# Output products beside the masked maxima of a relational graph layer, spread column tiles, a last bias in TensorE's sums

## The chip, the cores and the metric

The kernel runs on one core of a Trainium2 chip. The metric is the device time of one execution in microseconds (us), as the median of several runs; less is better.

## The reference, cut to what matters

1250 nodes with 768 features and 40000 edges of three relations pass through one block. A layer norm feeds two branches: a graph attention of two layers (RGAT), and a linear attention with 12 heads. Their sum is added to x, and an int8 feed-forward with its own layer norm is added to that.

```python
xn = _layernorm(x)
# graph branch, layer by layer (4 heads of 192, then 1 head of 768)
xr = einsum('nd,rdf->rnf', x, W)          # 3 relations
alpha = leaky_relu((xr[etype, dst] @ q) + (xr[etype, src] @ k), 0.2)
m = segment_max(alpha, dst); e = exp(alpha - m[dst])
a = e / (segment_sum(e, dst)[dst] + 1e-16)
out = segment_sum(a * xr[etype, src], dst) + b      # elu between the layers
# linear attention: phi(q), phi(k), sums over nodes
y = (phi(q) @ (phi(k)^T v)) / (phi(q) @ sum phi(k)) ; mix = y @ W_out + b_out
x = x + gnn(xn) + mix
x_int8 = clip(round(_layernorm(x) / 0.02), -128, 127)
x = x + (x_int8 @ weight_t) * 0.0002 + bias
```

## The kernel before

Nodes lie in 10 blocks of 128 (NB), features in 6 blocks of 128 (K6), and columns of a product in halves of 384 (CW). A product of one block of nodes with one chunk of weights is 18 matmuls of 384 columns in fp16: for each of six k, high by high, high by low and low by high (line 1948 for x, lines 1743 to 1745 for the others). A chunk's high part is made on ScalarE (ACT, `w_hi_part`), its low part on VectorE (DVE, `w_lo_part`, line 1309). Products alternate between PSUM banks 6 and 7. Every engine's order is written out by hand, with semaphores between engines; all DMAs go through the SyncE queue (SP), in the order of its program.

The stages, in the order of the program, with the lines that the text names:

- **K, V**: products of the linear attention, with the edge counts built beside them. For each of 60 windows of 21 target nodes DVE makes one-hot tiles (lines 1283, 1284) and TensorE (PE) multiplies them, 14 matmuls a window here (line 1756, `count_window`). ACT evicts a window, and SP stores it to `ct_d`.
- **Q**: six blocks of q (line 1838, 72 matmuls of 320 columns), three windows each. After a block's products come three tiles of "weights times q, k" (`wq_tile`, line 1817): 12 small matmuls each, of 8 columns in fp32 (2 columns for layer 2), whose sums W q and W k stay in PSUM. 36 tiles in all: 21 by the end of this stage, 15 in the next.
- **Attention**: for each of 10 node blocks, PE transposes (1870), multiplies by phi(k)^T v (1859), counts a window (1756, for eight of the blocks) and takes one or two tiles (1817). DVE normalises (1400 to 1409) and makes `yt_lo` (1422) and one-hots.
- **Node columns**: xn times (W q, W k) gives every node's scores (1885 to 1887, `node_columns`), transposed to rows (1895). It waits for `wqk_lo` of DVE (1431, 1433).
- **Output products**: 20 products of the attention with W_out (chunks C_O, C_O + 1). DVE has added the summed bias to x in SBUF (1439, ten operations), and then adds each product to X (1448); SP stores X to `acc_d` (626) from where the last stage reloads it. After ten of them `node_values` (1908) spreads the scores of two heads.
- **Maxima**: 30 iterations w (NW). SP has loaded the counts CT from `ct_d` in five bulk loads (461). ACT turns two windows into a mask (991), PE transposes it (1934, `mask_rows`, ten transposes), ACT evicts it (1002), and DVE reduces scores plus mask for each of four heads (1461). Beside that PE makes the 60 products of x with the relations' weights: 36 matmuls first (S0), then 32 an iteration (SW), and 84 after the last. ACT evicts them (983, `xr_part`), SP stores them to `xr_d` (467), and also stores every mask (637) and loads the chunks (478, 1152 KB each).
- **Softmax tables** on DVE, stored and spread by a DMA (`tq_d`, 663, `load_table`), the first head's rows loaded (`load_head`, 485), `b1_bc` loaded (673) when all products are stored. Then four heads of exponentials, weights and aggregation (1054, 1059, 1548, 1552, 1985). DVE waits for `b1_in` before the first of them.
- **Layer 2** likewise (five groups of columns, 2042, 2043), its outputs added to `ac` from `acc_d` and stored to `y_d`.
- **Feed-forward**: SP loads eight of ten blocks of y in one DMA (767, 3024 KB) when the last store has landed; DVE takes their statistics (1248) and quantises (1658, 1660, 1662) within the last group. After the last group PE transposes (2086) and multiplies (2076, 12 matmuls a block, ten blocks of 126 rows); GpSimd (POOL) adds the bias to fx (868), DVE scales and adds (1698, `block_out`), SP stores.

The code on which the order around the change rests:

```python
S0 = 2 * PM; SW = 32; S1 = S0 + SW * NW          # PM = 18 matmuls of a product
def wq_load(t):                                  # three buffers wt
    if t >= 3:
        sp.wait_ge(wt_used, t - 2)
def product_steps(q0, q1):                       # PE, matmul q of the x products
    ...
    pe.wait_ge(g_free, 6 * NB + n + 1)           # the bank of two products ago
def xr_part(n):                                  # ACT evicts product n
    act.wait_ge(ev_out[n % 2], 16 * (n // 2) + 16)
    act.wait_ge(g_done, 6 * NB + n + 1)
def block_out(b):                                # DVE, last stage
    dve.wait_ge(fb_done, b + 1)                  # POOL's bias add
    dve.wait_ge(f_mm, b + 1)
```

Of the kernel before, what the change touches and what calls it, by code (L numbers as in the profile page):

```python
# [13 lines left out]
F32 = mybir.dt.float32  # L14
F16 = mybir.dt.float16
# [9 lines left out]
P = 128  # L25
# [43 lines left out]
PW = 25  # L69
PM = 3 * K6  # L70
S0 = 2 * PM
SW = 32
S1 = S0 + SW * NW
LO_AT = (0, 6, 12, 17, 23)
# [10 lines left out]
def build(nc, x, src, dst, et, W1, q1, k1, b1, W2, q2, k2, b2, Wqkv, bqkv, Wo, bo, wf, bf, W1t, W2t, out):  # L85
    ctx = ExitStack()
    with ctx:
# [45 lines left out]
        zrow = keep("zrow", [P, QH], F16, 2)  # L133
# [12 lines left out]
        QF = place("QF", [P, K6, NPAD], F32, 159984)  # L146
# [3 lines left out]
        yt_hi = place("yt_hi", [P, K6, NPAD], F16, 98304)  # L150
        yt_lo = place("yt_lo", [P, K6, NPAD], F16, 98304 + 15360)
# [12 lines left out]
        b2_bc0 = place("b2_bc0", [P, D], F32, 98304)  # L164
# [11 lines left out]
        CT = place("CT", [P, NWN, NB, R, WN], U16, 127008)  # L176
        assert 127008 + NWN * QN * 2 <= 202900
# [3 lines left out]
        kbc = place("kbc", [P, H, ND], F32, 91936)  # L181
        tt_junk = [place(f"tt_junk{j}", [P, ND], BF16, 112096 + 2528 * j) for j in range(H)]
# [54 lines left out]
        al2_2 = place("al2_2", [32, R, 1, WD], F32, 118400)  # L237
        mx_2 = place("mx_2", [32, 1, WD], F32, 118912)
        mx2_2 = place("mx2_2", [32, 1, WD], F32, 119104)
        tq2 = place("tq2", [32, 2, R, WD], F32, 119296)  # L240
        mk2 = [place(f"mk2_{j}", [P, 1], F32, 120320 + 32 * j) for j in range(2)]
# [3 lines left out]
        bf_bc = place("bf_bc", [P, D], F32, 9216)  # L245
# [23 lines left out]
        y_d = scratch("y_d", (ND, D), F32)  # L269

# [43 lines left out]
        acc_out = sem("acc_out")  # L314
# [33 lines left out]
        ct_in = [sem(f"ct_in{j}") for j in range(2)]  # L348
# [46 lines left out]
        fx_in = sem("fx_in")  # L395
# [5 lines left out]
        fb_done = sem("fb_done")  # L401
# [21 lines left out]

        def products_of(w):

            return range((S0 + SW * w) // PM, (S0 + SW * (w + 1)) // PM)

# [14 lines left out]

        def block_windows(i):

            return range(W_A + i, min(W_A + i + 1, NWN))

        def block_tiles(i):

            t = WT_TILES // 2 + 3
            return range(t + 2 * i, t + 2 * i + 2) if i < 5 else range(t + 5 + i, t + 6 + i)  # L450
# [81 lines left out]
        def _(sp):  # L532
# [49 lines left out]
            sp.dma_start(b2_bc0[:, :], b2.unsqueeze(0).to_broadcast([P, D])).then_inc(bias_in, 16)  # L582

# [1538 lines left out]
```

## Time and profile before

| | |
|---|---|
| median of 3 runs | 1767.53 us (1766.63 to 1769.37) |
| the profiled execution | 1774.47 us, its span 1772.5 us |
| PE busy | 1629.0 us (92% of the span) |
| DVE busy | 1321.3 us (75%) |
| ACT busy | 772.9 us (44%) |
| POOL busy | 156.7 us (9%) |
| DMA | 175.75 MB, 99 GB/s over the span |
| chain that ended last | PE 66%, DVE 15%, issue 10%, DMA 4%, ACT 2% |

The profiled execution is 1.97 us longer than its span, and 6.94 us longer than the median of the runs. A busy PE isn't PE at its peak: the clock that was granted (PEclk) stands beside it, and the ends of matmuls are modelled. The two lines of the page that give DVE and the clock in 40 slices of 44.3 us:

```profile
DVE  8699876757723999948899898972774377777786
PEclk9999998988898999979999999989999899999988
```

The maxima lie in slices 13 to 17, the heads of layer 1 in 18 to 27, the feed-forward in the last one.

### The profile page before, as it was taken

To read this page: it belongs to the slowest core of one execution; us is meant where nothing else is said; L and a number is where in the kernel's file an instruction comes from. 1 tells how busy PE (TensorE), PEld (TensorE's weight loads), DVE (VectorE), ACT (ScalarE), POOL (GpSimd) and SP (SyncE) were. 2 spreads that over 40 slices of the span, in tenths; PEclk is the share of its full clock that TensorE was granted. 3 is DMA by queue.
4 is the path that set the end of the run, shared out by engine and by line. 5 is a ranking of instruction groups with operands and counts; after the bars stand their busy time and mean duration, and the time that the engine had idled before them with its cause. 6 is when DMAs were issued, how large, how long until landed. Compare 5 with 4: busy or idle time off the path is not lost.

```text
span 1772.5 us, 34725 instructions
## 1 busy us (share of the span) xinstructions
PE 1629.0 (92%) x10527; PEld 1194.4 (67%) x10528; DVE 1321.3 (75%) x2631; ACT 772.9 (44%) x1021; POOL 156.7 (9%) x248
## 2 busy tenths in 40 slices
PE   4999999999898999959999999989899799999966
PEld 3566667778654666559999999976555455555534
DVE  8699876757723999948899898972774377777786
ACT  3331112322103665358888898862211233333342
POOL 2000000000000000000000000000000133333334
PEclk9999998988898999979999999989999899999988
DMA  5111132233353453451004132133664621101202
GB/s 195 31 60 57 60 94 81 76 103 104 102 230 131 143 167 118 138 167 59 29 29 124 53 109 75 36 98 94 187 192 139 225 88 53 36 17 53 105 22 87
DMA packets 122054, 175.75 MB, mean 99 GB/s; under 512 B 13090, under 2 KB 95678, under 8 KB 121458
## 3 DMA queue, kind: packets, MB, share of 16 engines
q1 hardware_dynamic: 121970, 174.68, 30.9%
q8 instruction: 46, 0.75, 0.2%
q14 instruction: 38, 0.31, 0.1%
HBM read 117.78 MB, written 56.87 MB: 99 GB/s over the span
## 4 chain that ended last, share of the span: by engine, by line
PE 66%; DVE 15%; issue 10%; DMA 4%; ACT 2%; DVEq 1%; POOL 1%; SPq 1%; ACTq 0%; POOLq 0%
PE ps L1985 21%; PE ps L2043 7%; PE ps L2042 7%; PE ps L1756 6%; PE ps L1743 5%; PE ps L1744 5%; PE ps L1745 5%; DVE tt_junk L1461 5%; PE ps L1838 3%; PE ps L1817 3%; DVE w_lo L1309 1%; DVE oh_q L1283 1%; PE ps L1799 1%; PE ps L1859 1%; DMA xr_d<-ev 1%
## 5 line engine op out<-in xcount | busy, mean ns | idle before, releaser
L1985 PE MATMUL ps<-xrh,pf 128*128 (+1 forms) x2400 | 400.0, 330 | 24.2 <-DVE pf L1552 24.2
L1985 PEld LDWEIGHTS ps<-xrh,pf 128*128 128x128 f32 x2400 | 393.6, 191 | 30.7 <-issue 28.4
L1743 PE MATMUL ps<-w_hi,xt_hi 128*128 128x384 f16 x600 | 198.7, 331 | 22.4 <-DVE ev L1599 14.0
L2042 PE MATMUL ps<-x,ph 128*128 (+1 forms) x600 | 196.6, 328 | 20.6 <-POOL pl L857 15.1
L1283 DVE TENSOR_SCALAR oh_q<-pat,codeT,neg_w 125x630 f16<-125x630 uint16 x420 | 185.9, 443 | 39.3 <-PE ps L1756 29.3
L1552 DVE SCALAR_TENSOR_TENSOR pf<-vb,CT 128x1260 f32<-128x1260 f32 x120 | 175.8, 1468 | 35.0 <-PE ps L1985 35.0
L1744 PE MATMUL ps<-w_lo,xt_hi 128*128 128x384 f16 x600 | 198.5, 331 | 0.0
L1745 PE MATMUL ps<-w_hi,xt_lo 128*128 128x384 f16 x600 | 198.2, 330 | 0.0
L2043 PE MATMUL ps<-x,ph 128*128 (+1 forms) x600 | 198.0, 330 | 0.0
L1548 DVE SCALAR_TENSOR_TENSOR vb<-vb,tb 128x1260 f32<-128x1260 f32 x120 | 173.1, 1466 | 29.4 <-DMA b_bc<-in_L_gnn_b 19.7
L1461 DVE CUSTOM_DVE_ANT_0 tt_junk<-kbc,mb 126x1260 bf16<-126x1260 f32 x120 | 168.3, 1465 | 20.6 <-issue 19.9
L1059 ACT ACTIVATE vb<-qbc,kcol 128x1260 f32<-128x1260 f32 x120 | 161.0, 1345 | 39.2 <-DVE pf L1552 37.8
L1054 ACT ACTIVATE tb<-qbc,kcol_leak 128x1260 f32<-128x1260 f32 x120 | 159.8, 1343 | 27.9 <-DVE vb L1548 20.6
L1756 PE MATMUL ps<-oh_q,oh_p 125*128 125x315 f16 x840 | 140.5, 321 | 8.8 <-DVE oh_p L1284 8.3
L1121 ACT ACTIVATE ph<-p 128x252 f16<-128x252 f32 x150 | 61.9, 413 | 161.3 <-PE ps L2043 156.0
L857 POOL TENSOR_TENSOR pl<-p,ph 128x252 f16<-128x252 f32 x150 | 110.8, 739 | 200.8 <-ACT ph L1121 189.5
L1948 PE MATMUL ps<-w_hi,xt_hi 128*128 128x384 f16 x360 | 118.6, 329 | 7.5 <-ACT ev L983 7.4
L1756 PEld LDWEIGHTS ps<-oh_q,oh_p 125*128 125x128 f16 x840 | 87.3, 106 | 52.2 <-DVE oh_p L1284 7.1
L1948 PE MATMUL ps<-w_hi,xt_lo 128*128 128x384 f16 x360 | 118.5, 329 | 0.0
L1948 PE MATMUL ps<-w_lo,xt_hi 128*128 128x384 f16 x360 | 118.5, 329 | 0.0
L1599 DVE TENSOR_TENSOR ev<-ps,ev 128x384 f16<-128x384 f32 x60 | 32.8, 556 | 97.5 <-ACT ev L1108 95.2
L1284 DVE TENSOR_SCALAR oh_p<-iota_l,sloT 125x128 f16<-125x128 f16 x420 | 105.4, 251 | 0.0
(226 smaller groups left out, 2436.8 us busy)
## 6 DMA issues: line engine op xcount, KB each, us to landing
qbc<-tq_d SPq DMA_DIRECT2D x12, 1260.0 KB, 6.4
xr_d<-ev SPq DMA_DIRECT2D x60, 192.0 KB, 2.0
xrh<-xr_d SPq DMA_DIRECT2D x4, 2880.0 KB, 14.8
x_d<-ev SPq DMA_DIRECT2D x60, 192.0 KB, 2.3
mb_d<-mb SPq DMA_DIRECT2D x30, 310.1 KB
mb<-mb_d SPq DMA_DIRECT2D x30, 310.1 KB
wst<-in_L_gnn_W SPq DMA_DIRECT2D x8, 1152.0 KB, 8.7
x<-x_d SPq DMA_DIRECT2D x2, 3840.0 KB, 19.0
```

The costliest lines, as they stand in the source:

```text
L1283: dve.tensor_scalar(oh_q[0:ET, u, :], pat[0:ET, :], codes[:, k:k + 1], neg_w[0:ET, ds(w, 1)], ALU.subtract, ALU.is_equal)
L1461: dve.tensor_tensor_reduce(out=tt_junk[k][0:WK, :], in0=kbc[0:WK, h, :], in1=mb[w % 2][0:WK, :], scale=1.0, scalar=2 * BIG, op0=ALU.subtra ...
L1548: dve.scalar_tensor_tensor(vb[j][:, :], vb[j][:, :], 2.0, tb[j][:, :], ALU.min, ALU.max).then_inc(v_step, 1)
L1552: dve.scalar_tensor_tensor(pf[j][:, 0:ND].rearrange("p (w d) -> p w d", d=WN), vb[j][:, :].rearrange("p (w d) -> p w d", d=WN), 2.0, CT[:, ...
L1743: pe.matmul(ps[:, bank, 0:CW], a_hi, hi[:, k, :], start=(k == 0), stop=False)
L1744: pe.matmul(ps[:, bank, 0:CW], a_hi, lo[:, k, :], start=False, stop=False)
L1745: last = pe.matmul(ps[:, bank, 0:CW], a_lo, hi[:, k, :], start=False, stop=(k == K6 - 1))
L1756: last = pe.matmul(ps[:, bank + q, 0:QH], oh_p[0:ET, u, :], oh_q[0:ET, u, q * QH:(q + 1) * QH], start=start, stop=False, skip_group_check= ...
L1948: mm = pe.matmul(ps[:, 6 + n % 2, 0:CW], a[:, k, i * P:(i + 1) * P], w[:, k, :], start=(q % PM == 0), stop=(q % PM == PM - 1))
L1985: mm = pe.matmul(out[b], pf[j][:, b * DB:b * DB + P], x, start=(first and b % 2 == 0), stop=False, skip_group_check=True)
L2042: pe.matmul(ps[:, bank, 0:CW], p, cols(off, off + CW), start=start, stop=False, skip_group_check=True)
L2043: mm = pe.matmul(ps[:, bank + 1, 0:CW + n1], p, cols(off + CW, off + D + n1), start=start, stop=False, skip_group_check=True)
```

## The change

Four things, with what goes with them.

1. **Tiles spread.** `wq_tile` now stands singly inside the steps k of a q block (`step_tile`), at most one a step: 3, 5, 5, 5, 4 and 4 tiles in the six blocks (Q_TILES), 26 in the stage, and one for each of the ten attention blocks.
2. **x stored in the attention.** The ten additions of the bias to X are made by DVE in the last three q blocks, and SP stores all of X to `acc_d` during the attention blocks. X need not stay in SBUF; yt, CT, kbc and others move.
3. **Output products streamed.** All 80 products are one sequence (NE): six stand first (PRE), among node columns, rows and `node_values`; then 36 matmuls an iteration instead of 32; 252 matmuls after the last iteration instead of 84. For the 20 output products a ring of four buffers `oa` takes the place of X: SP loads a piece of `acc_d` (`load_o`), DVE adds the product (`o_out`), SP stores it (`store_o`). 15 of the 20 `o_out` stand between the reductions of iterations 0 to 7. CT is loaded in pieces (two windows, six, six, and then two an iteration), the chunks in six pieces of 192 KB, two an iteration.
4. **Last stage.** The feed-forward bias is split in three bf16 terms and added by one matmul with six rows per half (constants 8 and 4992, times 0.0002 is 1); POOL's ten additions go. Transposes and products of blocks 0 and 1 stand inside the last relation of the last group, in banks 4 to 7. fx comes in two loads of four blocks, the first without a wait for the stores of the fourth group. DVE's wait for `b1_in` moves to where b1 is first used.

```diff
-S0 = 2 * PM
-SW = 32
+S0 = PRE * PM
+SW = 2 * PM
 S1 = S0 + SW * NW
-LO_AT = (0, 6, 12, 17, 23)
+LO_AT = (3, 8, 13, 18, 23, 28)
+CT_EARLY = 14
...
+        Q_TILES = (0, 3, 8, 13, 18, 22, 26)
...
+        def load_o(sp, n):
+
+            c, i = n // NB, n % NB
+            if n >= 4:
+                sp.wait_ge(oa_out[n % 4], 16 * (n // 4))
+            sp.dma_start(oa[n % 4][:, :], acc_d[i * P:(i + 1) * P, c * CW:(c + 1) * CW]).then_inc(oa_in[n % 4], 16)
+
+        def store_o(sp, n):
+
+            c, i = n // NB, n % NB
+            sp.wait_ge(g_free, 4 * NB + n + 3)
+            sp.dma_start(acc_d[i * P:(i + 1) * P, c * CW:(c + 1) * CW], oa[n % 4][:, :]).then_inc(oa_out[n % 4], 16)
...
             for i in range(NB):
+                sp.wait_ge(xb_done, i + 2)
+                sp.dma_start(acc_d[i * P:(i + 1) * P, :], X[:, i, :]).then_inc(xs_out, 16)
...
             def store_product(n):
 
-                sp.wait_ge(g_free, 6 * NB + n + 3)
-                store_xr(sp, n // NB, n % NB, n % 2)
+                if n < 2 * NB:
+                    store_o(sp, n)
+                    if 4 <= n + 2 < 2 * NB:
+                        load_o(sp, n + 2)
+                else:
+                    sp.wait_ge(g_free, 4 * NB + n + 3)
+                    store_xr(sp, n // NB - 2, n % NB, n % 2)
...
+            def o_out(n):
+
+                dve.wait_ge(oa_in[n % 4], 16 * (n // 4 + 1))
+                dve.wait_ge(g_done, 4 * NB + n + 1)
+                dve.tensor_tensor(oa[n % 4][:, :], ps[:, 6 + n % 2, 0:CW], oa[n % 4][:, :], ALU.add).then_inc(g_free, 1)
...
             for w in range(NW):
+                if PRE - 1 + 2 * w < 2 * NB:
+                    o_out(PRE - 1 + 2 * w)
                 dve.wait_ge(mb_done, w + 1)
                 for k, h in enumerate(range(H - 1, -1, -1)):
+                    if k == 2 and PRE + 2 * w < 2 * NB:
+                        o_out(PRE + 2 * w)
...
             def block_out(b):
-                dve.wait_ge(fb_done, b + 1)
                 dve.wait_ge(f_mm, b + 1)
...
                 for hf in range(2):
+                    pe.matmul(ps[0:DB, 4 + 2 * j + hf, 0:CW], bone[:, 0:DB], brow[:, hf * CW:(hf + 1) * CW], start=True, stop=False)
                     for k in range(K6):
```

How the instructions move. On PE in the first q block, the tiles of weights times q, k (`qkn,wt`) before stand together between the last products (`xt`,`w`) and a window (`oh_q,oh_p`):

```order
L1838 MATMUL ps<-xt_hi,w_hi_80 128x320 x4
L1838 MATMUL ps<-xt_lo,w_hi_80 128x320 x4
L1838 MATMUL ps<-xt_hi,w_lo_82 128x320 x4
L1817 MATMUL ps<-qkn,wt_105 128x2x4 x6
L1817 MATMUL ps<-qkn,wt_106 128x2x4 x6
L1817 MATMUL ps<-qkn,wt_107 128x2x4 x6
L1756 MATMUL ps<-oh_q,oh_p 128x315 x8
```

The same place now (the lines are those of the changed file):

```order
L1885 MATMUL ps<-qkn,wt_110 128x2x4 x6
L1911 MATMUL ps<-xt_hi,w_hi_84 128x320 x4
L1911 MATMUL ps<-xt_lo,w_hi_84 128x320 x4
L1911 MATMUL ps<-xt_hi,w_lo_86 128x320 x4
L1885 MATMUL ps<-qkn,wt_111 128x2x4 x6
L1911 MATMUL ps<-xt_hi,w_hi_84 128x320 x4
L1911 MATMUL ps<-xt_lo,w_hi_84 128x320 x4
L1911 MATMUL ps<-xt_hi,w_lo_86 128x320 x4
L1824 MATMUL ps<-oh_q,oh_p 128x315 x8
```

Between two tiles there are now 12 matmuls of 320 columns. On DVE after the attention, before:

```order
L1422 TENSOR_TENSOR yt_lo<-ps,yt_hi 128x3x128 x2
L1309 TENSOR_TENSOR w_lo_83<-wst_79,w_hi_81 128x2304
L1431 TENSOR_TENSOR wqk_lo<-ps,wqk_hi 128x144
L1433 TENSOR_TENSOR wqk_lo<-ps,wqk_hi 128x36
L1436 COPY kcol<-ps 128x240
L1439 TENSOR_TENSOR X<-X,bsum 128x768 x10
```

and now, up to the first reductions (`tt_junk`), with the four ring buffers oa_133 to oa_136:

```order
L1490 TENSOR_TENSOR yt_lo<-ps,yt_hi 128x3x128 x2
L1499 TENSOR_TENSOR wqk_lo<-ps,wqk_hi 128x144
L1501 TENSOR_TENSOR wqk_lo<-ps,wqk_hi 128x36
L1508 TENSOR_TENSOR oa_133<-ps,oa_133 128x384
L1512 COPY kcol<-ps 128x240
L1371 TENSOR_TENSOR w_lo_87<-wst_83,w_hi_85 128x2304
L1508 TENSOR_TENSOR oa_134<-ps,oa_134 128x384
...
L1529 ISA tt_junk_142,mkt<-kbc,mb_139 126x1260
L1529 ISA mkt 126x1
L1529 ISA tt_junk_143,mkt<-kbc,mb_139 126x1260
L1529 ISA mkt 126x1
L1508 TENSOR_TENSOR oa_135<-ps,oa_135 128x384
```

The second low part stands behind `wqk_lo`, the ten additions to X are gone from here, and the additions of products stand between reductions. On SP, where bulk loads of CT and of a chunk stood ahead of the first products' stores, before:

```order
L610 DMA kq_d<-kq 24x1280
L478 DMA wst_78<-in_L_gnn_W 128x6x384
L461 DMA CT<-ct_d 128x5040
L461 DMA CT<-ct_d 128x12600 x2
L478 DMA wst_79<-in_L_gnn_W 128x6x384
```

stands now, at the start of iteration 0 of the maxima:

```order
L669 DMA mb_d<-mb_139 126x1260
L516 DMA acc_d<-oa_134 128x384
L510 DMA oa_136<-acc_d 128x384
L503 DMA wst_82<-in_L_gnn_W 128x384
L516 DMA acc_d<-oa_135 128x384
L510 DMA oa_133<-acc_d 128x384
L516 DMA acc_d<-oa_136 128x384
L510 DMA oa_134<-acc_d 128x384
L481 DMA CT<-ct_d 128x1260
```

Stores, reloads, mask stores and pieces of CT take turns in one queue.

## Rows read from the trace of the kernel before

**Rows 1.** Windows view, core 0: stretch, its us, busy by engine, clock, DMA share, GB/s
```profile
260.87:396.28 135.41, 135.41 (x931) 101.65 (x929) 90.05 (x294) 37.75 (x68) 1.88 (x1) 0.87 0.31 98
396.28:440.60 44.32, 42.37 (x297) 38.25 (x298) 33.49 (x118) 8.75 (x16) 0.00 (x0) 0.83 0.33 95
464.50:482.30 17.80, 13.40 (x227) 9.79 (x226) 12.69 (x16) 2.01 (x6) 0.00 (x0) 0.66 0.25 75
543.00:568.13 25.13, 18.45 (x100) 10.09 (x97) 8.31 (x11) 10.91 (x12) 0.00 (x0) 0.87 0.50 163
568.13:744.73 176.60, 174.32 (x1240) 111.09 (x1240) 172.14 (x294) 101.21 (x115) 0.00 (x0) 0.99 0.42 133
744.73:774.54 29.81, 8.41 (x52) 5.03 (x53) 9.11 (x20) 9.21 (x10) 0.26 (x4) 0.69 0.85 245
1726.20:1765.30 39.10, 29.14 (x180) 22.71 (x180) 29.45 (x40) 11.07 (x14) 21.54 (x14) 0.83 0.26 88
```

**Rows 2.** Timeline of PE, two stretches: start, us, line, operation, count
```profile
292.34 4.76 PE L1817 MATMUL ps<-qkn,wt 128*128 128x8 f32 x36
296.96 3.85 PE L1756 MATMUL ps<-oh_q,oh_p 125*128 125x315 f16 x14
...
424.16 2.81 PE L1859 MATMUL ps<-kvd,QF 128*128 128x130 f32 x12
...
441.29 1.51 PE L1859 MATMUL ps<-kvd,QF 128*128 128x130 f32 x12
442.64 2.08 PE L1756 MATMUL ps<-oh_q,oh_p 125*128 125x315 f16 x14
...
444.58 1.48 PE L1817 MATMUL ps<-qkn,wt 128*128 128x2 f32 x12
```

**Rows 3.** Timeline of DVE around the end of the attention
```profile
443.37 1.02 DVE L1409 TENSOR_TENSOR yn<-ps,rdn 128x384 f32<-128x384 f32 x2
...
449.38 1.02 DVE L1409 TENSOR_TENSOR yn<-ps,rdn 128x384 f32<-128x384 f32 x2
...
461.83 2.55 DVE L1309 TENSOR_TENSOR w_lo<-wst,w_hi 128x2304 f16<-128x2304 f32 x1
```

**Rows 4.** Timeline of PE, the node columns' first matmul
```profile
468.16 0.20 PE L1885 MATMUL ps<-wqk_hi,xt_hi 128*128 128x24 f16 x1 [3.65 <-DVE wqk_lo L1433]
```

**Rows 5.** Timeline of DVE in the output products
```profile
489.27 0.56 DVE L1448 TENSOR_TENSOR X<-ps,X 128x384 f32 x1 [2.39 <-PE ps L1745]
```

**Rows 6.** Timeline of ACT at the start of the maxima
```profile
567.58 0.49 ACT L983 ACTIVATE ev<-ps 128x384 f32<-128x384 f32 x1 [9.08 <-DMA xr_d<-ev]
```

**Rows 7.** Timelines of POOL, ACT and DVE before the first head
```profile
753.34 0.16 POOL L834 MEMSET xrh<- 128x30 f32 x1 [294.17 <-PE ps L1948]
...
764.77 2.58 ACT L1054 ACTIVATE tb<-qbc,kcol_leak 128x1260 f32<-128x1260 f32 x2 [5.71 <-DMA qbc<-tq_d]
...
770.16 2.85 DVE L1548 SCALAR_TENSOR_TENSOR vb<-vb,tb 128x1260 f32<-128x1260 f32 x2 [19.72 <-DMA b_bc<-in_L_gnn_b]
```

**Rows 8.** Timeline of DVE in the last group
```profile
1683.03 1.02 DVE L1248 BATCH_NORM_STATS2 stat<-fx 126x6 f32<-126x384 f32 x2 [4.75 <-DMA fx<-y_d]
```

**Rows 9.** Timelines of DVE and PE in the last stage
```profile
1743.36 2.04 DVE L1662 TENSOR_SCALAR fn<-fn 126x768 f32<-126x768 f32 x1
...
1746.95 0.56 DVE L1660 TENSOR_SCALAR fn<-fn 126x768 f32<-126x768 f32 x1
...
1764.29 1.02 DVE L1698 SCALAR_TENSOR_TENSOR fx<-ps,fx 126x384 f32<-126x384 f32 x2 [0.93 <-PE ps L2076]
...
1757.83 2.12 PE L2076 MATMUL ps<-wf,fqt 128*126 128x384 f16 x12
```

**Rows 10.** DMA issues: count, KB each, median us from issue to landing
```profile
wst<-in_L_gnn_W SPq DMA_DIRECT2D x24, 192.0 KB, 2.5
...
acc_d<-X SPq DMA_DIRECT2D x20, 192.0 KB, 2.8
...
CT<-ct_d SPq DMA_DIRECT2D x1, 315.0 KB, 3.2
```

More of the change, by code:

```diff
@@ L313, in build @@
         xb_done = sem("xb_done")
-        acc_out = sem("acc_out")
+        xs_out = sem("xs_out")
+        oa_in = [sem(f"oa_in{j}") for j in range(4)]
+        oa_out = [sem(f"oa_out{j}") for j in range(4)]
         qkn_in = sem("qkn_in")
@@ L347, in build @@
         ct_out = [sem(f"ct_out{j}") for j in range(2)]
-        ct_in = [sem(f"ct_in{j}") for j in range(2)]
+        ct_in = [sem(f"ct_in{j}") for j in range(4)]
         mt_done = sem("mt_done")
@@ L394, in build @@
         wf_done = sem("wf_done")
-        fx_in = sem("fx_in")
+        fx_in = [sem(f"fx_in{q}") for q in range(2)]
+        bf_step = sem("bf_step")
+        bf_st = sem("bf_st")
+        br_in = sem("br_in")
         f_step = sem("f_step")
@@ L1020, in _ @@
                     xr_part(n)
-            for n in range(S1 // PM, 2 * R * NB):
+            for n in range(S1 // PM, NE):
                 xr_part(n)
@@ L1394, in _ @@
                     count_part(W_Q + 3 * (3 * c + fb) + 3)
+                    if c == 1:
+                        for u in range(3):
+                            dve.tensor_tensor(sub(X, 3 * fb + u), sub(X, 3 * fb + u), bsum[:, :], ALU.add).then_inc(xb_done, 1)
+            dve.tensor_tensor(X[:, NB - 1, :], X[:, NB - 1, :], bsum[:, :], ALU.add).then_inc(xb_done, 1)
             def normalised(i):
@@ L1514, in head_scaled @@
                     dve.wait_ge(h_st, 32 * h)
+                elif blocks[0] == BLOCKS[0]:
+                    dve.wait_ge(b1_in, 16)
                 for b in blocks:
@@ L2044, in unit_products2, with ffn_product, ffn_transposes @@
                 mm.then_inc(mm_done, 1)
+            def ffn_product(b):
+                j = b % 2
+                pe.wait_ge(f_cp, b + 1)
+                if b >= 2:
+                    pe.wait_ge(f_out, 2 * (b - 1))
+                for hf in range(2):
+                    pe.matmul(ps[0:DB, 4 + 2 * j + hf, 0:CW], bone[:, 0:DB], brow[:, hf * CW:(hf + 1) * CW], start=True, stop=False)
+                    for k in range(K6):
+                        mm = pe.matmul(ps[0:DB, 4 + 2 * j + hf, 0:CW], fqt[j][:, k, 0:DB], wf16[:, k, hf * CW:(hf + 1) * CW],
+                                       start=False, stop=(k == K6 - 1))
+                mm.then_inc(f_mm, 1)
+            def ffn_transposes(b, bank):
+                pe.wait_ge(fq_done, b + 1)
+                for k in range(K6):
+                    last = pe.transpose(ps16[:, bank, k * DB:(k + 1) * DB], fq[b][0:DB, k * P:(k + 1) * P], ident16[0:DB, 0:DB])
+                last.then_inc(f_tr, 1)
             for g in range(NG):
```

354 lines of the change are left out of this document (184 added, 170 removed).

## The prediction

> **What bounds the kernel now.** I first read the page's chain that ended last: PE has 66% of it, DVE 15%, issue 10%. PE is busy 92% of the span, so time can go in two ways only: PE's idle time, or stretches in which PE is busy at less than full clock. The windows view shows where each lies [rows 1]: the columns to read are the length, PE's busy time, DVE's and the clock. The Q stage has no idle PE but a clock of 0.87; attention blocks 0 to 4 have both faults; the next four stretches lack 4.4, 6.7, 2.3 and 21.4 us of PE (length less busy); the last stage lacks 10.0. Then the timelines name what ended each wait [rows 2 to 9]. The heads of layer 1 and layer 2's groups are hardly edited, and are taken over unchanged.
>
> **Term A, Q stage.** The tiles of weights times q, k come in bursts of three, 36 small matmuls in 4.76 us, and the window behind such a burst takes 3.85 us where the same 14 matmuls take 2.08 later [rows 2]: half speed (1.2 of 2.4 GHz). The granted clock falls in or behind the burst. Seven bursts cost about 7 x 1.65 = 11.5 us that way (1.77 here, a little less in the others) (the clock of 0.87 would by itself allow 135.4 x 0.13 = 17.6, but the tiles' own time hardly depends on it). Single tiles between 12 matmuls each should not lower it; I take that from blocks 7 to 9 of the attention, where one tile of 1.48 us stands beside a window of 2.08 and 12 products in 1.51 (2.81 in the blocks with two tiles) [rows 2]. Against it stand five more tiles here, 5 x 1.35 = 6.7 us (a third of 4.0 to 4.8), and 1 us where DVE's ten additions to X, now under the last q blocks, hold up a one-hot: -11.5 + 6.7 + 1, **-4** (bounds +6, no clock gained and all added, and -8).
>
> **Term B, attention.** Blocks 0 to 4 with two tiles take 44.3 us [rows 1]: 4 to start and 5 of about 8. With one tile PE needs some 5.3 us a block at full clock, and DVE, which normalises and makes one-hots, 6.01 (449.38 less 443.37, from one block's `yn` to the next, in which DVE had no pause) [rows 3]. DVE becomes the limit: 4 + 5 x 6.0 = 34, **-10.3**; two later blocks that ran at 5.3 have a tile's worth more to share the clock with, +1. SP stores X here (3.8 MB at 95 GB/s already moving): nobody waits for these stores before the first reload. Net **-9.3** (bounds 0 and -12).
>
> **Term C, node columns to first head.** What goes, by stretch of rows 1:
> - 464.5 to 482.3: PE waits 3.65 us for `wqk_lo` [rows 4], because a `w_lo` of 2.55 stands ahead of it on DVE [rows 3]. It now stands behind. 4.4 less 0.8 for a wait of its length: -3.6.
> - 543 to 568: ACT waits 9.08 us for the store of `ev` [rows 6], which stands on SP behind two bulk CT loads and a whole chunk. These become pieces: -6.7, and 1 more for the clock of 0.87.
> - 568 to 744.7: its 2.3 us of idle.
> - 744.7 to 774.5: after the last product (the POOL memset at 753.34 marks it) ACT waits for `qbc` until 764.77, and DVE for `b_bc` until 770.16 [rows 7], the end of a queue that is 0.85 busy. Tables, head load and the new place of the `b1_in` wait now lie under 252 matmuls, 41 us at 0.163, instead of 84, 13.7. Left are an eviction of 0.5, four exponentials of 1.3 (half of 2.58), `vb` 1.43 (half of 2.85) and `pf` about as long, together about 8.8: -12.6.
>
> That is -26.2. The additions that leave the output stage free nothing on PE: there a product takes 2.95 us (2.39 waiting, 0.56 adding) [rows 5], which is 18 matmuls of 0.163, PE's own pace. All 80 products remain, and move only.
>
> What it adds: an iteration of maxima is 6.09 us now (176.6/29), 5.4 for 33 matmuls and 0.65 for ten transposes. With 36 matmuls PE needs 6.5. DVE spent 172.14 us in 29 iterations, with five `w_lo` of 2.55: (172.14 - 12.75)/29 = 5.5 for four reductions; two additions of 0.56 make it 6.6, with semaphores 6.8. So iterations 0 to 7 go at DVE's pace, 0.3 x 7.5 = 2.3 us more; the `w_lo` of iteration 3, 2.55 us, finds PE only one bank ahead, and I take 1.2 of it. Later iterations are PE's, 6.5 against 5.8 with a slack that takes each `w_lo` in. SP has also to wait for `tq` tables with stores queued behind it: products 71 to 79 stand there, and I take 2 us (nothing to 6). Net **-21** (bounds -12 and -26.2).
>
> **Term D, fx in two loads.** DVE's 4.75 us before the first statistics [rows 8] were one load of 3024 KB that waited for the last store of the fourth group. The first half now waits for older stores: **-4** (0 to -4.75).
>
> **Term E, last stage.** `fn` takes 2.04 us beside POOL's additions and 0.56 without [rows 9]; the 21.54 us of POOL [rows 1] go. A block is 12 matmuls of 384 columns in 2.12 us; two bias matmuls more, 14 x 0.163 + 0.33 for transposes = 2.6 a block. Two of ten blocks stand ahead, inside the last group, where PE waits for POOL's `pl` in any case. From the last group's end (about 1728, two us into the stretch) that is 8 x 2.6 = 21, plus about 2.5 of eviction: the last `block_out` ends near 1751.6 rather than at 1765.3 [rows 9]: **-13.5** (bounds -8, if DVE's work on quantising, 29.45 us in the stretch, takes PE's place as the limit, and -16).
>
> **Sum.** -4 - 9.3 - 21 - 4 - 13.5 = -51.8, say -51.5. Against the profiled execution of 1774.5 us this is 1723; the median of the runs lies 6.94 below that execution, so the forecast is **1716**. A measurement of this kernel tells about 0.2% (3.5 us) from no change.
>
> **A rule weighed.** The tables show 192 KB pieces landing 2.5 us after issue and ring stores of 2.8 [rows 10]. The Trainium skill, "DMA: Bandwidth & Descriptors", section on measured rates and its two cost components, says to batch transfers to at least 1 MiB, and that a transfer costs about 2.0 us fixed; that speaks against this change, which cuts 1152 KB chunks into six and adds a ring of 384-column pieces. By that figure a piece of 192 KB is estimated at 2.45 us, with which the trace agrees (2.5); six in turn would be 14.7 where one whole would be 4.7. What the rule would make of the time is the third rival below, in rows of this case.
>
> **Rivals.**
> 1. *The clock does not come back.* A tile itself, not the row of three, may be what lowers it, and there are five more in the Q stage. For it: the stretch 464.5 to 482.3 ran at 0.66 with no tile at all. Against it: the blocks with one tile [rows 2]. A and B shrink from -13.3 to -2: 1727 us. Chance 0.12.
> 2. *The ring is late.* In iterations 0 to 7 an iteration moves 2 x 192 KB in, 2 x 192 out, CT 315, the mask 310 out and chunk pieces, 230 on the mean: 1.6 MB in 6.5 us, 250 GB/s, where 133 are moved now and 245 at a DMA share of 0.85 [rows 1]. A buffer comes round in four products, 12.9 us, for store and reload; if in a full queue each of them takes as long as the longest wait now, 9.1 us [rows 6], a round is 5.3 longer, and four rounds (16 products) +21: 1737. Against it: 2.8 + 2.8 us unloaded [rows 10]. Chance 0.15.
> 3. *Slower: transfers in turn.* If each one waits for the one ahead, an iteration of the first eight is 2 x 2.8 + 2 x 2.8 for the ring, 3.2 for CT, 3.2 for the mask and 1.2 x 2.5 for pieces = 20 us rather than 6.5; 13.5 x 7.5 = +101, which gives 1817. The change turns from gain to loss where an iteration passes 6.5 + 51.5/7.5 = 13.4 us. For it: ring, CT and mask share SP's one queue. Against it: in 568 to 744.7 us two stores, a mask store and pieces would sum to over 8 us an iteration by the same count, and the pace is 6.09. Chance 0.03. (The rule of the Trainium skill, "DMA: Bandwidth & Descriptors", on small transfers points this way; no row here shows a queue in which they take full turns.)
> 4. *It does nothing of weight*, the gains at the node columns and the last stage being taken up by the next wait in both places, 1755 to 1775: 0.04.
>
> **The numbers.** The forecast as worked out has 0.66. Its bounds: A and B each 4 to 9 off, C 9, E 5.5, which do not fall together; the square sum is about 14. The range of **1702 to 1737** takes in rivals 1 and 2 and leaves out 3 and 4 and the ends of the forecast's own spread. Faster by over 0.2%: 0.66 + 0.12 + 0.15 and a quarter of rival 4, **0.94**; the same **0.02**, from rival 4; slower, rival 3 and the rest of rival 4, **0.04**.
>
> **What would show it.** Right: granted clock near 1.00 in Q and attention; attention blocks about 6.0 us apart; no wait of 3.65 us ahead of the node columns; iterations of maxima 6.5 to 6.8 us, and no addition waiting for a DMA; PE's gap between last product and first head about 9 us; no wait at the first fx statistics; `fn` near 0.56 throughout and a last stage of about 26 us rather than 39. Wrong: a clock under 0.95 in Q (A, B); DVE waiting for `oa` loads, or PE for banks with DVE idle (C); PE waiting for DVE's quantised blocks at the end (E).

## The result, and the profile after

The changed kernel takes 1757.15 us, the median of 18 runs (1752.94 to 1770.71), where the kernel before takes 1770.37 (18 runs, 1766.51 to 1775.91). The ratio is 0.9934, with a 95% interval of 0.9917 to 0.9951: faster, by 0.7%, about 12 us (the two medians are 13.2 apart), rather than the 51.5 us that were forecast. The forecast of 1716 was wrong, and so was its range, which ended at 1737. The profiled execution has a span of 1758.5 us, 14.0 less than before.

The windows view of the changed kernel, cut at the same places of the program as [rows 1] (columns as there): the Q stage, the attention up to the node columns' place, the products and maxima up to the first head, layer 1's end to layer 2's first group, the groups, and the last stage.

```profile
260.90:414.59 153.69, 135.13 (x992) 100.92 (x991) 96.75 (x303) 37.08 (x68) 2.76 (x6) 0.94 0.33 100
414.60:473.00 58.40, 52.71 (x422) 46.23 (x420) 55.20 (x184) 15.11 (x29) 2.20 (x9) 0.97 0.47 141
473.00:768.16 295.16, 274.86 (x1960) 170.73 (x1959) 206.63 (x351) 128.92 (x143) 0.26 (x4) 0.96 0.58 176
1170.30:1402.30 232.00, 202.14 (x1334) 123.08 (x1334) 117.99 (x246) 60.60 (x103) 2.08 (x11) 0.93 0.51 154
1402.30:1716.70 314.40, 303.56 (x1823) 178.29 (x1824) 241.41 (x524) 121.18 (x306) 116.18 (x164) 0.98 0.20 66
1716.70:1758.50 41.80, 30.80 (x179) 19.79 (x177) 22.40 (x49) 10.71 (x13) 1.48 (x4) 0.90 0.27 92
```

The same stretches of the kernel before:

```profile
260.80:396.14 135.34, 135.34 (x933) 101.55 (x931) 90.12 (x294) 37.75 (x68) 1.88 (x1) 0.87 0.31 98
396.14:464.50 68.36, 64.96 (x482) 58.66 (x480) 54.46 (x182) 15.21 (x29) 2.20 (x9) 0.87 0.31 92
464.50:774.50 310.00, 274.50 (x1959) 170.86 (x1958) 215.74 (x360) 126.36 (x142) 0.26 (x4) 0.93 0.48 158
1177.20:1405.90 228.70, 200.57 (x1334) 122.66 (x1334) 117.42 (x245) 60.47 (x102) 1.42 (x10) 0.94 0.53 156
1405.90:1721.60 315.70, 300.61 (x1797) 176.33 (x1797) 241.28 (x523) 119.36 (x304) 116.46 (x165) 0.98 0.19 67
1721.60:1772.50 50.90, 29.96 (x185) 23.02 (x183) 33.82 (x51) 12.68 (x16) 21.54 (x14) 0.81 0.23 76
```

Set beside the terms of the prediction, these lengths give:

| stretch | forecast | change of its length |
|---|---|---|
| A, Q stage | -4 | **+18.4** |
| B, attention | -9.3 | -10.0 |
| C, node columns to first head | -21 | -14.8 |
| heads (402.7 to 402.1) and the way to layer 2's groups | 0 | +2.7 |
| D, groups of layer 2 | -4 | -1.3 |
| E, last stage | -13.5 | -9.1 |
| sum | -51.8 | -14.1 |

Nearly the whole shortfall of 38 us lies in A (22), C (6) and D with E (7). The first row is the one to read twice: PE is busy for as long as before (135.13 and 135.34 us), at a higher clock (0.94 for 0.87), which has paid for the five tiles more; but 18.6 us of idle time have come into a stage that had none. The waits view of PE names them, for the changed kernel in the Q stage (in the kernel before it is empty there):

```profile
PE ps L1824 <- DVE oh_p L1346: 12.3, 12, 5.6
PE ps L1911 <- DVE q_t L1451: 5.4, 5, 1.1
```

The timeline of PE shows where one block of q hands over to the next, and the end of the last block:

```profile
277.17 0.43 PE L1911 MATMUL ps<-xt_hi,w_hi 128*128 128x320 f16 x2
278.69 0.77 PE L1911 MATMUL ps<-xt_hi,w_hi 128*128 128x320 f16 x2 [1.09 <-DVE q_t L1451]
...
284.27 0.72 PE L1824 MATMUL ps<-oh_q,oh_p 125*128 125x315 f16 x4 [0.24 <-DVE oh_p L1346]
285.82 0.99 PE L1824 MATMUL ps<-oh_q,oh_p 125*128 125x315 f16 x6 [0.83 <-DVE oh_p L1346]
...
312.86 1.23 PE L1911 MATMUL ps<-xt_hi,w_hi 128*128 128x320 f16 x4
...
317.40 0.70 PE L1911 MATMUL ps<-xt_hi,w_hi 128*128 128x320 f16 x4
...
410.47 2.26 PE L1824 MATMUL ps<-oh_q,oh_p 125*128 125x315 f16 x8 [5.64 <-DVE oh_p L1346]
```

and the timeline of DVE at such a place what it does meanwhile:

```profile
377.92 1.01 DVE L1451 TENSOR_SCALAR q_t<-ps,bq_col 128x320 f32<-128x320 f32 x2 [3.02 <-PE ps L1911]
379.62 0.49 DVE L1456 SCALAR_TENSOR_TENSOR QF<-q_t,q_m 128x320 f32 x1 [0.69 <-ACT q_m L996]
...
383.44 0.49 DVE L1456 SCALAR_TENSOR_TENSOR QF<-q_t,q_m 128x320 f32 x1 [0.37 <-ACT q_m L996]
384.49 0.45 DVE L1345 TENSOR_SCALAR oh_q<-pat,codeT,neg_w 125x630 f16<-125x630 uint16 x1 [0.56 <-issue]
```

The two lines at 312.86 and 317.40 are the same four matmuls at half and at full clock. In windows of one or two us the granted clock falls to 0.50 three times between 265 us and the stage's end: at about 313, at about 364, both behind a seam with such waits, and within the wait of 5.64 us. The other profiles of kernels with this order of tiles (after_again, c_pieces, d_onefx, e_rows) show such falls too, at two to four places, the last wait among them. So the waits seem to cost twice, as idle time and as clock; b_cover below bears on it.

A block of q ends in 6.6 us of evictions (377.92 to 384.49), in turns of DVE and ACT, and only then come the one-hots of the next window, 3.6 us more. PE has a window of 1.9 us to do before it needs q's bank again, and then two steps k before it needs the one-hots: 4.6 us with a tile between them, as in most blocks, 3.3 without. Before the change it had a window and three tiles at the seam (the place between two blocks), together 7.8 us, which is more than the evictions take:

```profile
380.26 4.08 PE L1817 MATMUL ps<-qkn,wt 128*128 128x8 f32 x36
384.20 3.71 PE L1756 MATMUL ps<-oh_q,oh_p 125*128 125x315 f16 x14
```

That is the theory that the experiments test: the tiles in a row lost clock and at the same time were the cover of DVE's evictions.

In C, the timelines of SP's queue and of ACT in the 252 matmuls behind the last iteration:

```profile
722.36 0.36 SPq L523 DMA_DIRECT2D xrh<-xr_d  x1
722.77 6.37 SPq L712 DMA_DIRECT2D tq_d<-tq  x1
729.19 1.71 SPq L487 DMA_DIRECT2D xr_d<-ev  x1
735.38 0.36 SPq L520 DMA_DIRECT2D qbc<-tq_d  x1
```

```profile
735.56 0.49 ACT L1043 ACTIVATE ev<-ps 128x384 f32<-128x384 f32 x1 [10.06 <-DMA xr_d<-ev]
742.39 1.01 ACT L1043 ACTIVATE ev<-ps 128x384 f32<-128x384 f32 x2 [6.33 <-DMA xr_d<-ev]
```

The first head's 2880 KB are asked for at 722.36, and land 11.5 us later. What SP does next is held up in three ways. Its issue of the softmax tables' store (`tq_d`, 118 KB) lasts 6.37 us, and that store lands after 12.6 us. The store of a product, 192 KB, is issued only at 729.19 and lands after 6.3 us: that is the first of ACT's waits. Then SP waits for `tq_d` to land before it loads the table (`qbc`, 1260 KB, 735.38), and the next product's store stands behind that load: the second wait. ACT can't evict, and PE stops twice, 5.34 and 2.06 us.

In the last stage, the weight loads and DVE's outputs of the changed kernel:

```profile
1738.21 0.13 PEld L2111 LDWEIGHTS ps<-brow,bone 6*126 6x126 bf16 x1
1738.51 0.84 PEld L2113 LDWEIGHTS ps<-wf,fqt 128*126 128x126 f16 x6 [0.17 <-issue]
1739.63 0.13 PEld L2111 LDWEIGHTS ps<-brow,bone 6*126 6x126 bf16 x1 [0.28 <-issue]
```

```profile
1737.98 1.02 DVE L1766 SCALAR_TENSOR_TENSOR fx<-ps,fx 126x384 f32<-126x384 f32 x2 [2.15 <-PE ps L2113]
1741.15 1.02 DVE L1766 SCALAR_TENSOR_TENSOR fx<-ps,fx 126x384 f32<-126x384 f32 x2 [2.15 <-PE ps L2113]
```

A block takes 3.17 us, not 2.6, and PE is what DVE waits for.

### The profile page after: what moved, and what is told of

It is laid out like the page before. It is cut to its first block, busy times and chain, and to the rows that moved or that the text cites. A ratio compares the mean times of both kernels' runs of the same rounds, so it can differ in the third digit from the quotient of the medians.

```text
span 1758.5 us, 34402 instructions
## 1 busy us (share of the span) xinstructions
PE 1621.5 (92%) x10547; PEld 1179.7 (67%) x10548; DVE 1308.4 (74%) x2631; ACT 774.4 (44%) x1021; POOL 138.1 (8%) x245
## 4 chain that ended last, share of the span: by engine, by line
PE 75%; DVE 10%; issue 5%; DMA 3%; ACT 3%; DVEq 2%; POOL 1%; SPq 1%; ACTq 0%; POOLq 0%
PE ps L2044 22%; PE ps L1995 12%; PE ps L2102 7%; PE ps L2101 7%; PE ps L1811 5%; PE ps L1813 4%; PE ps L1812 4%; PE ps L1824 4%; PE ps L1911 2%; PE ps L1885 2%; DVE oh_q L1345 2%; DVE oh_p L1346 1%; PE ps L2113 1%; PE ps L1980 1%; DMA xr_d<-ev 1%
## 5 line engine op out<-in xcount | busy, mean ns | idle before, releaser
L2101 PE MATMUL ps<-x,ph 128*128 (+1 forms) x600 | 196.5, 327 | 16.8 <-POOL pl L921 10.8
L1824 PE MATMUL ps<-oh_q,oh_p 125*128 125x315 f16 x840 | 132.1, 304 | 23.7 <-DVE oh_p L1346 23.1
L1824 PEld LDWEIGHTS ps<-oh_q,oh_p 125*128 125x128 f16 x840 | 80.9, 99 | 66.3 <-DVE oh_p L1346 20.1
L1811 PEld LDWEIGHTS ps<-w_hi,xt_hi 128*128 (+1 forms) x600 | 59.7, 99 | 68.7 <-issue 32.4
## 6 DMA issues: line engine op xcount, KB each, us to landing
xrh<-xr_d SPq DMA_DIRECT2D x4, 2880.0 KB, 14.8
```

The source lines that it names most:

```text
L1811: pe.matmul(ps[:, bank, 0:CW], a_hi, hi[:, k, :], start=(k == 0), stop=False)
L1824: last = pe.matmul(ps[:, bank + q, 0:QH], oh_p[0:ET, u, :], oh_q[0:ET, u, q * QH:(q + 1) * QH], start=start, stop=False, skip_group_check= ...
L2101: pe.matmul(ps[:, bank, 0:CW], p, cols(off, off + CW), start=start, stop=False, skip_group_check=True)
```

## The experiments

Four edits of the changed kernel ran beside each other, each on one place.

**a_bursts** puts the tiles of weights times q, k back as they were, and nothing else:

```diff
-                        for t in step_tile(3 * c + fb, k):
-                            wq_tile(t)
...
+                    for t in range(3 * (3 * c + fb), 3 * (3 * c + fb) + 3):
+                        wq_tile(t)
                     count_window(wa + 2, 6, *of_w[2])
...
+            for t in range(18, 21):
+                wq_tile(t)
             count_window(W_A - 1, 6, *of_w)
```

> The changed kernel with its column tiles put back as before (three in a row ahead of each q block's last window, three ahead of the window between the stages, two in each of the first five attention blocks); the rest of the change stays. Theory C (cover): the row of tiles and the slow window behind it hid DVE's evictions of q, about 6.6 us, and its one-hots behind them; spread tiles expose them. Then the Q stage falls from 153.7 us back to about 136 (135.4 plus 1 for the additions), with no PE wait in it, the attention grows from 58.4 back to about 68, and the kernel gets some 8 us faster than the changed one: about 1749, 0.988 of before. Theory K (clock, the prediction's term A): the bursts cost clock and hide nothing; the Q stage grows by 11.5 less 6.7 us to about 158, the attention to 68, the kernel comes to about 1771, as before.

Measured: 1745.82 us (1742.82 to 1749.34), ratio to before 0.9853 (0.9829 to 0.9877). Its windows for Q stage and attention:

```profile
260.80:399.00 138.20, 138.20 (x930) 104.83 (x929) 98.45 (x303) 37.70 (x68) 2.82 (x6) 0.85 0.30 95
399.00:466.30 67.30, 62.22 (x483) 56.16 (x482) 55.41 (x184) 15.61 (x31) 2.21 (x9) 0.91 0.51 152
```

No idle PE in the Q stage, and 15.5 us less than in the changed kernel, in spite of a clock of 0.85. So one part of the change, taken by itself, was a loss: with the tiles left alone the rest gives 26 us, twice what all of it gave. The prediction's theory wanted 1771. The Q stage is 2.9 us longer than before, where DVE's ten additions to X were given 1 (138.20 is PE busy throughout, so this shows as slower matmuls, not as a wait; the runs don't divide it).

**b_cover** keeps single tiles, 26 of them in the stage, and moves two of each block's to its seam:

```diff
+                    for t in step_tile(3 * c + fb, 6):
+                        wq_tile(t)
                     count_window(wa + 2, 6, *of_w[2])
+                    for t in step_tile(3 * c + fb, 7):
+                        wq_tile(t)
```

> The changed kernel with single tiles as now and 26 of them in the Q stage, but of each block's tiles one stands ahead of the block's last window and one behind it, at the cost of inner steps. Theory C: these two, 2.7 us, push the next block's first bank and first window back by as much as DVE needs: the waits of 1.1 us for q's bank go, those for one-hots fall from about 1.1 to below 0.5 a block, the clock stays at 1.00, the wait of 5.6 us ahead of the attention falls to about 4; the Q stage comes to about 141 us and the kernel to about 1745. Theory K: single tiles next to a window lower the clock as rows do (under 0.95 in the Q stage), and nothing is gained: 1757.

Measured: 1735.34 us (1731.82 to 1736.96), ratio 0.9797 (0.9775 to 0.9819), 22 us below the changed kernel. Windows and PE's wait in the Q stage:

```profile
260.90:390.10 129.20, 125.51 (x989) 98.42 (x987) 96.23 (x302) 36.87 (x68) 2.97 (x6) 0.99 0.37 118
390.10:450.20 60.10, 54.21 (x423) 48.14 (x421) 57.03 (x187) 15.61 (x31) 2.21 (x9) 0.92 0.45 137
```

```profile
PE ps L1830 <- DVE oh_p L1352: 3.7, 3, 3.0
```

The stage takes 129.2 us, 6.1 less than before; the prediction's term A said 4 less (131.4). The expectation of 141 was too high: it left PE's busy time about as it was, and that fell too. Both halves of the theory hold: the clock is 0.99 with single tiles, at a window as well as between products, and the waits are 3.7 us instead of 17.7. Of the 24.5 us between this stage and the changed kernel's, 14.9 are idle time and 9.6 are PE's busy time for the same instructions (125.51 us for 135.13): with the gaps their falls of the clock are gone. About 2 us of the 9.6 lie at the stage's start, where the half clock left from the stage before ended at 260.4 here and at 264.6 there, which no edit explains.

**c_pieces** cuts the load of the first head:

```diff
-            load_head(sp, 0)
...
             for n in range(S1 // PM + 5, NE):
                 store_product(n)
+                p = n - S1 // PM - 5
+                if p < 6:
+                    r, b0 = p // 2, NB // 2 * (p % 2)
+                    sp.dma_start(xrh[0][:, r, b0:b0 + NB // 2, 0:HD], xr_d[0, r, b0:b0 + NB // 2].rearrange("b p n -> p b n")).then_inc(xrh_in[0], 16)
```

> The changed kernel with the first head's rows (2880 KB) loaded in six pieces, one behind each of six later products' stores, instead of one load ahead of the last ten stores. Theory Q (queue): ACT's waits of 10.1 and 6.3 us for the stores of ev, and PE's of 7.4 us for ACT, are those stores standing behind the 14.8 us of the load; in pieces both fall under 1 us and the last product ends 7 us earlier; the kernel comes to 1750. Rival (bandwidth): store and load share what the queue moves however they are cut, and the waits stay at 5 us or more in sum: 1755 to 1757.

Measured: 1745.47 us (1741.03 to 1746.17), ratio 0.9842 (0.9819 to 0.9866), 12 us below the changed kernel. The waits views of PE (first product to first head) and of ACT:

```profile
PE ps L2047 <- DVE pf L1625: 8.8, 1, 8.8
PE ps L1998 <- DVE oa L1511: 2.4, 1, 2.4
PE ps L1998 <- DVE yt_lo L1493: 1.2, 1, 1.2
```

```profile
ACT ev L1046 <- DMA xr_d<-ev: 5.8, 2, 4.3
```

ACT still waits twice for stores, 5.8 us where it was 16.4, but PE doesn't wait for ACT any more: two banks hold so much. From the first output product to the last product it is 275.0 us, 9.7 less than in the changed kernel (284.67); 7.4 of this is PE's idle time and the rest the matmuls behind it, the clock going from 0.97 to 0.98. The expectation's "under 1 us" failed: the two stores that ACT waits for land 7.1 and 6.2 us after their issue, one behind the table load of 1260 KB and the other behind a piece of 480 KB. The `tq_d` store takes 0.35 us to issue and lands after 3.1 us. The rival's own sign, waits of 5 us or more in sum, is met by ACT's 5.8; against it stand its time, 1755 to 1757, and PE's waits, which are gone. The edit cuts the load and also moves it behind the tables' store; which of the two does it was not run. The Trainium skill, "DMA: Bandwidth & Descriptors", section on queues, rings and completion order, states that on each DMA engine the descriptors of one row are consumed in ring order; the changed kernel's trace agrees: the load issued at 722.36 landed at 733.9, the `tq_d` store behind it at 735.4, and the store issued at 729.19, for which ACT waited, at 735.5.

**e_rows** makes the bias product's contraction 128 rows long, rows 6 on being zero in the constants:

```diff
-        bone = keep("bone", [2 * 3, P], BF16, 2)
+        bone = keep("bone", [P, P], BF16, 2)
-        brow = place("brow", [2 * 3, D], BF16, 9216)
+        brow = place("brow", [P, D], BF16, 9216)
+            sp.dma_start(brow[6:P, :], bf_d[0:1, :].to_broadcast([P - 6, D])).then_inc(br_in, 16)
+            pool.affine_select(out=bone[:, :], in_=bone[:, :], compare_op=ALU.is_gt, fill=0.0, base=6, pattern=[[0, P]], channel_multiplier=-1)
```

> The changed kernel with the bias matmul over 128 rows instead of six (rows 6 to 127 of the constants are zero), so two bias matmuls a block as now. A block of the last stage takes 3.17 us now where 2.6 was forecast, since the weight load behind each bias matmul begins 0.17 to 0.28 us late. Theory S (shape): a matmul of six rows and one of 128 don't overlap, and with 128 rows a block takes 2.6 us: 1757 less 7 x 0.57, about 1753. Theory D (type): it is the change of bf16 to fp16 between them; then a block stays at 3.17 and the time at 1757.

Measured: 1753.5 us (1747.53 to 1764.2), ratio 0.9921 (0.9892 to 0.995), which doesn't by itself part from the changed kernel's. The profile does: the last stage is 37.6 us instead of 41.8, and the weight loads follow each other:

```profile
1713.00:1750.60 37.60, 26.02 (x180) 20.74 (x177) 22.24 (x49) 10.62 (x13) 1.48 (x4) 0.88 0.30 103
```

```profile
1736.04 0.14 PEld L2114 LDWEIGHTS ps<-brow,bone 128*126 128x126 bf16 x1
1736.20 0.95 PEld L2116 LDWEIGHTS ps<-wf,fqt 128*126 128x126 f16 x6
```

```profile
1737.54 1.02 DVE L1769 SCALAR_TENSOR_TENSOR fx<-ps,fx 126x384 f32<-126x384 f32 x2 [1.59 <-PE ps L2116]
1740.14 1.02 DVE L1769 SCALAR_TENSOR_TENSOR fx<-ps,fx 126x384 f32<-126x384 f32 x2 [1.59 <-PE ps L2116]
```

A block is 2.60 us, the forecast's value. The type is the same bf16 as before the edit, so it is the shape: 128 rows instead of six cost nothing, and save 0.57 us a block. The Trainium skill, "TensorE: Matmul & The Clock Gate", section on what each phase is for, says that a weight load is pulled ahead of a running matmul when the row groups don't conflict or it goes to the background buffer, and that the number of rows doesn't matter to its time. The duration of the load agrees (0.13 and 0.14 us for 6 and 128 rows); that the load behind the six-row matmul began 0.17 us late is not what the rule by itself would let one expect, and why it did so stays open.

The second group ran on one chip too, but for i_four, which ran later and on another (the kernel before took 1774.72 us there), and is compared by its ratio.

**after_again** is the changed kernel, unedited.

> The changed kernel once more, unedited, beside the edits on one chip: 1757 us, 0.993 of before. It also tells whether the stretch from layer 1's last product to layer 2's first (232.0 us in its profile, 228.7 before) is longer because of the change (again 232) or by chance (228 to 232).

Measured: 1758.97 us (1754.5 to 1760.9), ratio 0.9935 (0.9912 to 0.9958), as at first. The way from layer 1 to layer 2's groups:

```profile
1167.70:1395.70 228.00, 199.59 (x1334) 121.72 (x1333) 117.83 (x246) 60.37 (x102) 2.08 (x11) 0.95 0.52 157
```

It is 228.0 us here, against 232.0 and, before, 228.7. The 3.3 us in the table are not seen again: they are chance between executions, as far as these profiles show, and no part of the change.

**d_onefx** loads fx in one DMA again:

```diff
-            for q in range(2):
...
+            for b in range(2):
+                sp.wait_ge(ot_out[b], 16 * (NG - 1))
+            sp.dma_start(fx[0:DB, 0:8, :], y_d.rearrange("(b p) n -> p b n", p=DB)[:, 0:8, :]).then_inc(fx_in[0], 16)
```

> The changed kernel with fx loaded in one DMA of eight blocks behind the fourth group's last store, as before. The prediction's term D: the statistics wait 4.75 us again, PE's wait for POOL's pl in the last group goes from 3.2 back to about 6.8 at its longest, and the time grows by 4 to 1761. Rival: that wait was taken over by another, and one load costs nothing: 1757.

Measured: 1760.32 us (1756.78 to 1768.06), ratio 0.9946 (0.9929 to 0.9963) beside 0.9935 of the unedited one: not told apart. In the profiles DVE's wait ahead of the statistics is 4.55 us, with two loads 1.18 (the changed kernel's first profile) and 2.93 (after_again). PE's waits for `pl` over the groups sum to 14.1 us, with two loads to 10.8 and 11.0, and the longest is 6.6, with two loads 3.2 and 4.9. The groups take 317.8 us, with two loads 314.4 and 315.9. So a part of the DVE wait of [rows 8] goes, about 3 us less of waiting reach PE, and the groups get 2 to 3 us shorter, where two profiles of one kernel differ by 1.5. That this moves the kernel's time is not shown.

**f_three** has the edits of b_cover, c_pieces and e_rows together.

> The changed kernel with three repairs at once: the tiles that cover the q evictions (22 us off in the runs before), the first head in pieces (about 10) and the bias over 128 rows (4). If they are independent, as the theory has it (three places, each on PE's path), the kernel comes to 1757 - 22 - 10 - 4 = 1721, which is near the 1716 that was forecast for the change. If they hide one another, or the run-to-run differences had a share in them, 1728 or more.

Measured: 1718.07 us (1716.28 to 1718.91), ratio 0.9704 (0.9681 to 0.9728). The windows of its Q stage, attention, products to the last one, and last stage:

```profile
260.00:389.70 129.70, 126.02 (x993) 98.87 (x991) 96.89 (x304) 37.11 (x68) 3.12 (x6) 0.99 0.37 119
389.70:449.80 60.10, 53.01 (x423) 46.51 (x420) 57.04 (x187) 15.50 (x31) 2.21 (x9) 0.95 0.45 137
449.80:724.70 274.90, 272.36 (x1958) 170.21 (x1958) 200.65 (x344) 120.53 (x133) 0.00 (x0) 0.98 0.60 184
1677.60:1714.60 37.00, 24.81 (x179) 19.91 (x177) 22.20 (x49) 10.63 (x13) 1.49 (x4) 0.94 0.31 105
```

Each stretch has the length that its edit alone gave, so the three add up (40.9 us from 1758.97, where 22, 12 and 4 make 38), and together they close the gap to the forecast: the ratio is 52 us off the kernel before, for 51.5. That the sum comes out so well is in part luck, since A now gives 2 us more than was forecast, and the groups of layer 2, where D was to gain 4 us, give less.

**g_five** adds two more. DVE writes block 0's output before the last group's output, and the attention's first product stands ahead of the window:

```diff
+            block_out(0)
             quantise(EARLY)
...
-            count_window(W_A - 1, 6, *of_w)
             pe.wait_ge(q_out, 2 * 3 * NRG + 2)
...
             weighted(0)
+            count_window(W_A - 1, 6, *of_w)
```

> The three repairs and two more: the last stage's first output (block 0) is added by DVE in the last group, as soon as its product is there, instead of behind the statistics of blocks 8 and 9, so that the product of block 2 does not wait 2.57 us for its bank; and the attention's first product stands ahead of the window between the stages, whose one-hots come late. About 2.5 and 1.5 us: 1717. If DVE's addition now delays the weights of the last group or its output, less: 1720.

Measured: 1716.06 us (1715.28 to 1716.76), ratio 0.9692 (0.9669 to 0.9716). The profiled spans are the same (1714.9 and 1714.6), and PE merely waits elsewhere: 1.28 us for q and 3.88 for `yn` around the moved window, 2.2 for ACT's `fqt` where 2.57 were for a bank.

**i_four** is g_five without the moved window:

> The three repairs and the early first output, without the attention's first product ahead of the window. In the run before, that order brought nothing: PE's waits around it were 1.28 and 3.88 us (3.04, 0.30 and 2.01 without it), and the attention ran at a clock of 0.89 rather than 0.93. If so, this is 1 to 2 us below the version with both: 1715. If the first output does nothing either (its bank wait of 2.57 us became 2.2 us for ACT's fqt), 1718 as with three.

Measured: 1718.06 us (1713.17 to 1720.16), ratio 0.969 (0.9673 to 0.9707). The three versions are not told apart. Neither small edit is shown to bring anything.

## Why the prediction was wrong, point by point

- **The reading of what bounds it** (idle PE, or PE at half clock) was right, and the gains were sought in the right places. What failed were three things that the change put in there: gaps of PE at the seams of the q blocks, the place of the first head's load, and the shape of the bias matmul.
- **Term A** failed, by 22 us, and far outside its bounds (+6 and -8). The step is "-11.5 + 6.7 + 1": it counted what the row of tiles cost PE, and not what PE's time in it was for. What was missing is a fourth summand, the wait for DVE when the cover is gone: 18.6 us of idle PE. The other 3.7 are in PE's busy time, 135.13 us where the sum has 131.4: the clock fell again behind the waits (0.94 over the stage; the sign "a clock under 0.95 in Q" came, for another reason than the one given). The profile of before could have told of the wait. DVE was 67% busy in the stage [rows 1], which reads as slack, but its work comes in one lump of 10.2 us at each block's end, and PE's 7.8 us of tiles and window stood just there. With a cover kept, the stage gives more than the term (b_cover: -6.1 for -4), and by other sizes: PE's busy time falls by 9.8 us although 6.7 us of tiles came in, so that the clock and what else the spread changed gave about 16.5, not 11.5, and 3.7 us of wait stand against it. The summand of 1 us for DVE's additions wasn't measured by itself.
- **Term B** held: -10.0 for -9.3, and the blocks stand 6.0 us apart, at DVE's pace, as [rows 3] had it (`yn` to `yn`).
- **Term C** was 6 us off. The gap between last product and first head is 8.9 us for 8.8, iterations take 7.0 us while the ring runs and 6.4 later, for 6.8 and 6.5 (ACT's evictions of masks 1, 8 and 29 start at 517.06, 566.34 and 701.12), and no addition waits for a ring load. What failed is the last of its steps, "SP has also to wait for `tq` tables with stores queued behind it ... I take 2 us (nothing to 6)". SP did wait there, 4.5 us for `tq_d` to land, and a store stood behind it. But the wait was mis-sized because the head load's 2880 KB ahead of it all were counted only as hidden under the 252 matmuls: they held up the issue and the landing of `tq_d` and the store behind it, and without them in that place the products end 9.7 us earlier. The step on the `w_lo` of iteration 3, 1.2 us, measured 2.4.
- **Term D** was mis-sized, or hidden: it took all of DVE's wait as time. DVE's wait fell from 4.75 us to 1.18 and, in the other profile, 2.93; beside d_onefx PE's waits are 3 us and the groups 2 to 3 us shorter.
- **Term E** was mis-sized by one price. "14 x 0.163" takes a bias matmul at the price of its neighbours; it costs that and 0.28 us more, 0.57 a block, 4.6 over eight blocks. Block 0's product and transposes, 3 us, lie in the groups' length now (303.56 us busy for 300.61) and not under their waits, which is most of what D's row lacks. Block 1's product, which was to stand ahead too, ran from 1717.43, right behind the group's last matmul. Block 2 waited 2.57 us for its bank; its product began 6.5 us after the end of the group's last matmul, where the sum has 5.6 (1722.4 to 1728), so that of this wait 1 us at most is on top of what was reckoned. The additions of POOL are gone and `fn` takes 0.56 throughout, as said.
- **The rivals**: none of them happened as described. The measured time lies in the band of the fourth, "it does nothing of weight" (1755 to 1775, chance 0.04), but not by its mechanism: the gains at the node columns and in the last stage came, 14.8 and 9.1 us, and 18.4 us were lost in the Q stage. The clock came back with single tiles, the ring was never late, transfers didn't take turns. From 502 to 560 us, where the ring ran, the windows view has 204 GB/s moved, for 133 in the maxima before, without a wait of the ring, and pieces of 192 KB landed in 3.2 us for 2.5. The rule of the Trainium skill, "DMA: Bandwidth & Descriptors", section on measured rates, on batching to at least 1 MiB, which was weighed there, didn't decide anything; where a transfer did harm, it was the largest one, whole. A rival of the kind "a wait takes the place of the one removed", with DVE's evictions named, was the one that was missing, and the range had no room for it.

## What to carry to other kernels

Before work is taken from a place where it looks wasteful, ask what the other engines do in that time. In this kernel a lump of evictions at the end of a block needed as much of TensorE's work behind it, whatever the mean busy share said. Filler was cheap exactly there, so try the seams before the inside when you spread work. A large load that nobody needs yet does not belong in a queue ahead of small stores that free a buffer; let it follow them, in pieces.

## What the runs showed of the hardware

- A matmul of six rows between matmuls of 128 rows kept the weight loads from overlapping: 0.17 us ahead of the next load and 0.28 ahead of the one for the next bias matmul, 3.17 us a block. The same matmul padded with zeros to 128 rows took no longer, and the block 2.60 us (e_rows).
- Single tiles of 12 small fp32 matmuls left the granted clock at 0.99 over the stage (b_cover); three in a row, with no idle time of PE at all, brought it to 0.85 (a_bursts) and 0.87 (before), at the same kind of neighbours. Single tiles with waits of 0.2 to 1.1 us at the seams and one of 5.64 had 0.94 (the changed kernel).
- Behind the 2880 KB load SP's next issue, of a 118 KB store, lasted 6.37 us (0.35 without the load ahead of it), that store landed after 12.6 us (3.1), and a 192 KB store issued 6.8 us after the load landed after 6.3. ACT waited 10.06 us for it. With the load in six pieces of 480 KB behind later stores the longest such wait was 4.3 us in c_pieces and 4.2 in f_three, and PE waited for none.
